# A third buffer for x, gathered two tiles ahead, and x's rows stored in another order

## The reference

```
xi = x[:, pi, :]            # 2048 x 496 x 64
xj = x[:, pj, :]
proj = einsum('bpd,pod->bpo', xi, W)
return proj * xj            # 2048 x 496 x 64
```

## Time and profile before

| | |
|---|---|
| median of 3 runs | 676.4 us |
| the profiled execution: time | 674.19 us |
| the profiled execution: span of the trace | 672.4 us |
| TensorE, matmul | 578.1 us busy, 86% |
| VectorE | 412.5 us, 61% |
| GpSimd | 404.4 us, 60% |
| ScalarE | 206.4 us, 31% |
| DMA queue q1 (SyncE's), share of the 16 engines | 94.0% |
| DMA queue q0 (the gathers) | 4.9% |
| DMA queue q10 (ScalarE's) | 0.4% |
| bytes moved | 285.20 MB, 424 GB/s |

### The profile page before, as it was taken

One profiled execution on the slowest core, in us unless ns is written; L12 is line 12 of the kernel. 1 busy time (PEld: TensorE's weight loads), 2 busy tenths in 40 slices (PEclk: granted clock), 3 DMA queues, 4 the chain that ended last, 5 costly groups with the idle time before them and its releaser, 6 DMA issues.

```text
span 672.4 us, 6957 instructions
## 1 busy us (share of the span) xinstructions
PE 578.1 (86%) x2704; PEld 346.3 (51%) x2704; DVE 412.5 (61%) x528; ACT 206.4 (31%) x257; POOL 404.4 (60%) x242
## 2 busy tenths in 40 slices
PE   5999897989898897889989889898989989889840
PEld 4565554646465464545636455464645546455420
DVE  1777485666666676566756656675666756656640
ACT  3333332333332232333323232242332323232210
POOL 1859467574766667476565756756566575756530
PEclk9999898998899899988979899898999989999775
DMA  8999999999999999999999999999999999999996
GB/s 339 394 430 438 442 414 448 428 426 434 433 426 439 422 448 418 443 420 437 426 421 436 424 442 429 434 426 425 431 436 424 428 418 436 435 427 431 438 427 293
DMA packets 12128, 285.20 MB, mean 424 GB/s; under 512 B 1680, under 2 KB 1808, under 8 KB 3536
## 3 DMA queue, kind: packets, MB, share of 16 engines
q1 hardware_dynamic: 9728, 270.28, 94.0%
q0 software_dynamic: 2016, 13.76, 4.9%
q10 hardware_dynamic: 368, 0.98, 0.4%
HBM read 25.89 MB, written 260.05 MB: 425 GB/s over the span
## 4 chain that ended last, share of the span: by engine, by line
DMA 56%; PE 27%; DVE 7%; POOL 5%; ACT 1%; issue 1%; SPq 0%; DVEq 0%; POOLq 0%
DMA out_dram<-staged 51%; PE proj L334 25%; DVE staged L384 7%; POOL staged L259 5%; DMA x_sb<-x_dram,rows_sb 3%; ACT staged L300 1%; DMA x_sb<-x_dram 1%; PE proj L312 1%; DMA ident_sb<-ident_dram 1%; PE proj L357 1%; ACT x_t L274 0%; POOL x_sb L242 0%; SPq L208 0%; DVEq L147 0%; POOLq L241 0%
## 5 line engine op out<-in xcount | busy, mean ns | idle before, releaser
L334 PE MATMUL proj<-w_sb,x_t 64*128 64x512 f32 (+7 forms) x2432 | 543.6, 551 | 54.6 <-DVE staged L384 53.2
L384 DVE TENSOR_TENSOR staged<-proj,x_sb 128x1024 f32<-128x1024 f32 (+7 forms) x528 | 412.5, 827 | 235.2 <-PE proj L334 161.9
L259 POOL TENSOR_TENSOR staged<-staged,x_sb 128x1024 f32<-128x1024 f32 (+4 forms) x224 | 389.7, 1754 | 201.3 <-ACT staged L300 198.6
L334 PEld LDWEIGHTS proj<-w_sb,x_t 64*128 64x128 f32 x2432 | 314.3, 194 | 280.5 <-issue 134.1
L300 ACT ACTIVATE staged<-proj 128x1024 f32<-128x1024 f32 (+4 forms) x224 | 174.0, 788 | 398.9 <-PE proj L334 304.6
L274 ACT ACTIVATE x_t<-proj 128x1024 f32<-128x1024 f32 x32 | 31.1, 1021 | 37.6 <-PE proj L312 37.6
L312 PE MATMUL proj<-ident_sb,x_sb 128*128 128x128 f32 x256 | 32.5, 282 | 7.4 <-DMA x_sb<-x_dram,rows_sb 7.3
L242 POOL DMA_INDIRECT x_sb<-x_dram,rows_sb x14 | 14.6, 1040 | 39.4 <-DVE staged L384 21.6
L312 PEld LDWEIGHTS proj<-ident_sb,x_sb 128*128 128x128 f32 x256 | 28.7, 144 | 13.0 <-DMA x_sb<-x_dram,rows_sb 11.4
L357 PE MATMUL proj<-ident_sb 128*128 128x128 f32 x16 | 3.6, 418 | 5.5 <-DMA ident_sb<-ident_dram 5.5
L357 PEld LDWEIGHTS proj<-ident_sb 128*128 128x128 f32 x16 | 3.3, 224 | 5.5 <-DMA ident_sb<-ident_dram 5.5
## 6 DMA issues: line engine op xcount, KB each, us to landing
out_dram<-staged SPq DMA_DIRECT2D x15, 5504.0 KB
out_dram<-staged SPq DMA_DIRECT2D x15, 5472.0 KB, 26.0
out_dram<-staged SPq DMA_DIRECT2D x15, 4896.0 KB, 26.7
out_dram<-staged SPq DMA_DIRECT2D x1, 3520.0 KB, 18.8
out_dram<-staged SPq DMA_DIRECT2D x1, 3008.0 KB
out_dram<-staged SPq DMA_DIRECT2D x1, 2784.0 KB, 22.6
out_dram<-staged SPq DMA_DIRECT2D x1, 2496.0 KB
out_dram<-staged SPq DMA_DIRECT2D x1, 2112.0 KB, 24.2
```

Source lines behind the costliest of these rows:

```text
L259: last = nc.gpsimd.tensor_tensor(product, product, x_sb[tile.parity][:, j * dim:(j + n) * dim], ALU.mult)
L334: last = nc.tensor.matmul(proj[b][h][:, at:at + width], x_t[tile.parity][half, i // 2, :], w_sb[half, col:col + width], start=True, stop=True)
L384: last = nc.vector.tensor_tensor(staged_part(item, i, j, n), proj[b][h][:, at:at + n * dim], x_sb[tile.parity][:, j * dim:(j + n) * dim], ...
```

## The change

- `x_sb` has three buffers in place of two, and a tile's x is loaded two tiles ahead. `x_t` has one buffer in place of two.
- "turn" becomes two items of 8 transposes each: "turn_low" (fields 0 to 15 of the next tile) before step 16, and "turn_high" (fields 16 to 31 of this tile) before step 8. A tile has 23 items in place of 22 (tile 0 and the last tile 22).
- The table of items is made ahead for all tiles (`schedule`), and TensorE's code is written out for all 16 tiles.
- ScalarE loads no x. The rows that the main gather leaves out are 16 to 19 alone (`APART`), and GpSimd gathers these four with an indirect DMA of their own, before step 3; the main gather (124 rows) comes before step 10. In tile 0 GpSimd waits for the row table before step 3.
- On the host, the rows of x of tiles 2 to 15 are put into DRAM in another order: the eight rows that one DMA engine takes follow each other.

```
-TURN_BEFORE = 18
-LOAD_BEFORE = 3
-GATHER_BEFORE = 4
+TURN_LOW_BEFORE = 16
+TURN_HIGH_BEFORE = 8
+APART_BEFORE = 3
+GATHER_BEFORE = 10
+LOW_PAIR = {"turn_low": 0, "turn_high": 8}
-SKIPPED = range(12, 20)
+APART = range(16, 20)
...
+    def tile_items(number):
+        for s in range(len(steps)):
+            if s == TURN_HIGH_BEFORE and number > 0:
+                yield "turn_high"
+            if s == TURN_LOW_BEFORE and number < tiles - 1:
+                yield "turn_low"
+            yield s
...
-        x_sb = [sb(f"x_sb{h}", [P, fields * dim]) for h in range(2)]
-        x_t = [sb(f"x_t{h}", [P, fields // 2, P]) for h in range(2)]
+        x_sb = [sb(f"x_sb{h}", [P, fields * dim]) for h in range(3)]
+        x_t = sb("x_t", [P, fields // 2, P])
...
+            def load_apart(number):
+                h, _ = loads_of(number)
+                if number >= len(x_sb):
+                    _, b, use = schedule[number - len(x_sb)][-1]
+                    pool.wait_ge(emptied[b][1], use + 1)
+                    pool.wait_ge(pool_scaled[group_of[pool_steps[-1]]], number - len(x_sb) + 1)
+                at = tiles + number
+                nc.gpsimd.indirect_dma_start(
+                    x_sb[h][APART.start:APART.stop, :], None, x,
+                    bass.IndirectOffsetOnAxis(ap=rows_sb[0:len(APART), at:at + 1], axis=0),
+                    bounds_check=batch - 1, oob_is_err=False).then_inc(x_apart_loaded[h], 16)
+            def load_x(number):
+                h, loads = loads_of(number)
+                pool.wait_ge(x_apart_loaded[h], 16 * loads)
+                nc.gpsimd.indirect_dma_start(
+                    x_sb[h][:], None, x,
+                    bass.IndirectOffsetOnAxis(ap=rows_sb[:, number:number + 1], axis=0),
+                    bounds_check=batch - 1, oob_is_err=False).then_inc(x_loaded[h], 16)
             def emit(tile):
                 for item, b, use in items(tile):
-                    if item == GATHER_BEFORE and not tile.first and not tile.last:
-                        if tile.number == 1:
+                    if item == APART_BEFORE and tile.number + 2 < tiles:
+                        if tile.first:
                             pool.wait_ge(rows_loaded, 16)
-                        load_x(tile)
+                        load_apart(tile.number + 2)
+                    if item == GATHER_BEFORE and tile.number + 2 < tiles:
+                        load_x(tile.number + 2)
...
-            def turned_out(b, use, to):
+            def turned_out(b, use, low, count):
                 for h in range(2):
                     act.wait_ge(filled[b][h], use + 1)
-                    nc.scalar.activation(x_t[to][:, h * (UNIT // P):(h + 1) * (UNIT // P), :].rearrange(
-                        "p k b -> p (k b)"), proj[b][h][:], ACT.Copy).then_inc(emptied[b][h], 1)
-            def load_skipped(tile):
...
+                    at = low + h * (count // 2)
+                    nc.scalar.activation(x_t[:, at:at + count // 2, :].rearrange("p k b -> p (k b)"),
+                                         proj[b][h][:, 0:count // 2 * P], ACT.Copy).then_inc(emptied[b][h], 1)
...
-            each_tile(pe, emit)
+            every_tile(emit)
...
+    p = np.arange(P)
+    engine, turn = 8 * (p >> 6) + ((p >> 2) & 7), 4 * ((p >> 5) & 1) + (p & 3)
+    x_rows = np.asarray(r_x).reshape(-1, P, fields * dim).copy()
+    for t in range(2, len(x_rows)):
+        numbers[:, t] = t * P + 8 * engine + turn
+        x_rows[t][8 * engine + turn] = x_rows[t].copy()
+    rows[:, :numbers.shape[1]] = numbers
+    rows[APART.start:APART.stop, :numbers.shape[1]] = NO_ROW
+    rows[:len(APART), numbers.shape[1]:] = numbers[APART.start:APART.stop]
```

More of the change, by code:

```diff
@@ L75, with __init__ @@
 class Tile:
-    def __init__(self, number, parity, half, last=False):
-        self.number, self.parity, self.half, self.last = number, parity, half, last
-        self.first = isinstance(number, int) and number == 0
+    def __init__(self, number, tiles):
+        self.number, self.first, self.last = number, number == 0, number == tiles - 1
 def field_pair_project(nc, x, w, ident, rows, out, fields, dim):
@@ L86, in field_pair_project @@
     w_at, w_ends = w_columns(fields, dim)
-    assert 2 * dim == P and fields == 32 and tiles % 2 == 0 and tiles >= 4
+    assert 2 * dim == P and fields == 32 and tiles >= 4
+    assert all(i >= fields // 2 for s in range(TURN_LOW_BEFORE, len(steps)) for unit in steps[s] for i, _, _ in unit)
     assert all(2 * c == fields * dim for c in (UNIT,))
[L91 to L94, removed]
+    def tile_items(number):
[5 more added lines that the diff above has]
+            yield s
+    schedule, used = [], 1
+    for t in range(tiles):
+        here = list(tile_items(t))
+        schedule.append([(item, (used + n) % 2, (used + n) // 2) for n, item in enumerate(here)])
+        used += len(here)
     def items(tile):
-        for n, item in enumerate(last_tile if tile.last else whole_tile):
-            yield item, (1 + n) % 2, tile.number * per_tile + (1 + n) // 2
+        return schedule[tile.number]
     pool_steps = [s for s in range(len(steps) - 1) if s % 3 != 2]
@@ L136, in every_tile, with loads_of @@
         for t in range(tiles):
[L137 to L145, removed]
+            emit(Tile(t, tiles))
+    def loads_of(number):
+        return number % len(x_sb), (number + 1) // len(x_sb)
     with ExitStack() as ctx:
@@ L269, in _ @@
             act.dma_start(ident_sb[:], ident).then_inc(ident_loaded, 16)
-            def turned_out(b, use, to):
+            def turned_out(b, use, low, count):
                 for h in range(2):
                     act.wait_ge(filled[b][h], use + 1)
-                    nc.scalar.activation(x_t[to][:, h * (UNIT // P):(h + 1) * (UNIT // P), :].rearrange(
-                        "p k b -> p (k b)"), proj[b][h][:], ACT.Copy).then_inc(emptied[b][h], 1)
-            def load_skipped(tile):
[L279 to L286, removed]
+                    at = low + h * (count // 2)
+                    nc.scalar.activation(x_t[:, at:at + count // 2, :].rearrange("p k b -> p (k b)"),
+                                         proj[b][h][:, 0:count // 2 * P], ACT.Copy).then_inc(emptied[b][h], 1)
             def emit(tile):
                 for item, b, use in items(tile):
[L290 to L293, removed]
+                    if item in LOW_PAIR:
+                        turned_out(b, use, LOW_PAIR[item], fields // 4)
                     elif item in pool_steps:
@@ L329, in project @@
                 for h in range(2):
-                    if not (tile.first and use == 0):
+                    if use:
                         pe.wait_ge(emptied[b][h], use)
@@ L334, in project @@
                         last = nc.tensor.matmul(
-                            proj[b][h][:, at:at + width], x_t[tile.parity][half, i // 2, :],
+                            proj[b][h][:, at:at + width], x_t[half, i // 2, :],
                             w_sb[half, col:col + width], start=True, stop=True)
@@ L340, in emit @@
                 for item, b, use in items(tile):
-                    if item == "turn":
-                        if tile.first:
+                    if item in LOW_PAIR:
+                        of = tile.number + (item == "turn_low")
+                        if of == 1:
                             pe.wait_ge(x_second_loaded, 16)
                         else:
-                            loads = tile.half + 1 if tile.parity else tile.half
-                            pe.wait_ge(x_loaded[1 - tile.parity], 16 * loads)
-                            pe.wait_ge(x_rest_loaded[1 - tile.parity], 16 * loads)
+                            x_h, loads = loads_of(of)
+                            pe.wait_ge(x_apart_loaded[x_h], 16 * loads)
+                            pe.wait_ge(x_loaded[x_h], 16 * loads)
                         for h in range(2):
                             pe.wait_ge(emptied[b][h], use)
-                            turn(b, 1 - tile.parity, h)
+                            turn(b, of, h, LOW_PAIR[item], fields // 4)
                     else:
```

38 lines of the change are left out of this document (14 added, 24 removed).

## The result

The changed kernel takes 678.87 us (median of 14 runs, 677.50 to 681.18) against 676.18 us for the kernel before (14 runs, 674.01 to 676.90): ratio 1.0047 of the mean times, 95% interval 1.0037 to 1.0058, so 3.2 us slower (the medians differ by 2.7). I had said 677, +0.8 us in the sum. The interval lies wholly above 1.003: what came is "slower by over 0.3%", to which I had given 0.35, and not "no change", which had 0.42. The profiled execution has a span of 675.8 us in place of 672.4. At 677.65 us it is the second fastest of its 14, so the profile shows about a us less than the median lost.

What follows compares the result with a forecast made beforehand. The most heavily loaded DMA engine was taken to set the time: 674.19 - 3.3 (rows) + 1.3 (code) + 2.8 (wait) = 675.0, plus 2.2 from profiled execution to median is 677.2, said as 677. The range was 672 to 689 us.

Steps and rivals of the forecast that it cites:

- The bound: Whole kernel: the most heavily loaded DMA engine sets the time; compute may come 13 us late before an engine runs dry.
- x's rows by engine: Loads of x: the six engines with 9 rows a tile do 0.75 fewer, -3.3 us, bounds nothing to 4.4.
- the four rows go round the engines: Four-row gather: assumed to fall on other engines each time; the rival, always the same four, gave 680.5, chance 0.1.
- TensorE written out: TensorE's code for all 16 tiles: 14 more code packets hold DMA engines, +1.3 us, bounds 0.9 and 2.7.
- GpSimd's wait in tile 0: Before step 3: waiting for the row table delays the second store and the queue runs dry, +2.8 us, bounds 2.0 and 3.5.
- the forecast's own range: Whole kernel: 674.5 to 679.5 us, from the ranges of the rows, code and gap terms, not all at one end.
- Order in DRAM: Gathers of x: the new row order was taken as worth 0, with a possible gain of 0.8 us.
- 14 us of bursts: Order of rows, other side: a slow burst losing about 1 us in each of 14 gathers; none showed in tile 8.
- Third buffer, x two tiles ahead, halves: TensorE, GpSimd and ScalarE: waits removed and small work added all lie under the 13 us of cover, costed at 0.
- The overloaded engine: Rival on x's rows: an engine gets back rows it can't carry, 687 to 694 us, middle 690, chance 0.25.
- The faster rival: Whole kernel: balance and order pay and tile 0's gap is short, giving 673.4 us, chance 0.2.

Runs made afterwards that it cites:

- e4_apart_only: The kernel before, with ScalarE loading no x and GpSimd gathering rows 16 to 19 by an indirect DMA of their own: 672.33 us, ratio 0.9952.
- e6_wait_only: The kernel before, with one more wait: GpSimd waits for the row table before step 3 of tile 0; 680.76 us, ratio 1.0071.

## Why the prediction was right and wrong

*The bound* was right for the two kernels compared: the chain goes from store to store in both, and the engines are full. It is less safe than I took it to be. In e4_apart_only and the three kernels that have two buffers for x and the wait, 49 to 63% of the chain from 100 to 620 us is the gather of x, and in e6_wait_only TensorE waits 61.5 us for it. With three buffers it never does.

*x's rows by engine*, -3.3: right in size, -3.2 alone. That it comes from the six engines with 9 rows is shown in part: the idle time at the end fell by 1.6 us of the 3.0 gained, the rest came from all engines at once, and ScalarE's DMA went with the same edit.

Whether the four rows go round the engines stays open. Each gather of four rows moves 32 packets (e4_apart_only, 54 to 56 us):

```profile
q0 software_dynamic: 32, 0.03, 4.7%
```

A tile's gather of all 128 entries moves 144 packets, 16 more than its entries. By the same count the small one has 16 entries, 12 of them empty; with eight rows apart the queue has the same 2464 packets. The rule of the Trainium skill ("DMA: Bandwidth & Descriptors", Why a DMA increments its semaphore by 16 and not by 1) on a cursor that goes round is for a DMA on fewer than 16 engines. No run here shows that it bears on this one.

*TensorE written out*, +1.3: not contradicted. Sixteen packets came for the 14 of the sum. Alone the change cost +0.7 us with 0 inside the interval; the kernels with the loop (0.9952, 0.9950) and with the code written out (0.9956, 0.9950) can't be told apart.

*GpSimd's wait in tile 0*, +2.8: the step that failed, by its size. Its chain held: table at 30.2 predicted, gather issued at 31.34; second store predicted at 35.6, issued at 36.67; queue dry predicted from 33.6 to 36.6, idle from about 34 to 37. The hole of 3.0 us is the size that I took. But "it goes straight into the end, since from there on the engines are full again" was wrong in the second half. Full is not the same as fast: the wait costs 6.1 us in the changed kernel, 4.8 in the kernel before and 5.3 in the one with four rows apart. With the sizes measured one by one the sum is -3.2 + 0.7 + 6.1 = +3.6 for a measured +3.2. The time of 678.9 still lay inside the forecast's own range, 674.5 to 679.5, because that range was wide and not because it held this cost: the bounds of the term, 2.0 and 3.5, did not.

*Order in DRAM*, 0: right, within 1 us, in all four pairs. The 14 us of bursts that I had named as the other side never came.

*Third buffer, x two tiles ahead, halves*: cost 0, right as far as 1 us can be told. The change with the wait gone (0.9956) equals the two-buffer kernel with the four rows apart (0.9952).

*The rivals.* The overloaded engine had 0.25 and an argument from the DMA share: two engines with 17.6 us less work were not silent early. The observation stands, the conclusion that the engine is slow in itself does not: given its rows back, it carried them. The faster rival's 673.4 is near what the change gives without the wait, 0.9956 x 676.2 = 673.2, but by luck: it counted on a short gap, a gain from the order and 2 us around the gathers, and none of the three was there.

What stays open is why the packets are slower after the hole, and whether one reason holds for both kinds of kernel: stores between 45 and 57 us with three buffers, gathered rows through the whole run with two. The hole lets all 16 engines start again at one moment, and a reason in their being in step would fit the rest of 2.5 to 4 us in the table, but nothing here sets them in step without a hole, so it is argued and not shown. Of the 6.1 us, 3.0 are the hole and 1.1 lie from 38 to 80 us; the other 2 us show in no stretch of the traces (1.2 of them lie between the changed kernel's profiled execution and its median).

## What to carry to other kernels

Where DMA is the bound, count the work of each DMA engine, not the mean: that count (9 rows on six engines, made 8.25 on all) foretold the 3.2 us, though the trace shows only half of them as a more even end. Then look at what each newly moved instruction waits for in the first tile: a gather one tile earlier met a table loaded last, and this one wait ate twice the whole gain. The best version here is the smallest edit: the kernel before with four rows gathered apart, 672.3 us, 0.9952 of the time before; the change with its gathers a few steps later or its table loaded first does as well.

## What the hardware showed that I had not expected

A hole of 1 to 3 us in all DMA engines' work was followed by slower packets at a full share: 420 for 431 GB/s over 42 us in the changed kernel, most of it in stores that took 41.4 us a MB in place of 37.3 from 45 to 57 us; 427 for 431 over 560 us in the kernel before with the wait alone, with gathered rows at 0.355 us in place of 0.314. In six pairs of kernels the wait cost 2.5 to 4 us more than the hole it made.
